# Self attention with one turn per entry, operands through a DRAM scratch, and the maxima rows laid in by transfer

## The reference, cut to what matters

```python
# 4 batch entries, 512 tokens, 128 features, 16 heads of 8
for l in range(N_LAYERS):                      # 4 layers
    h = rmsnorm(x, n1[l])
    q, k, v = jnp.split(h @ Wqkv[l].T + bqkv[l], 3, axis=-1)
    q = apply_rope(split_heads(q, H), cos, sin)
    k = apply_rope(split_heads(k, H), cos, sin)
    o = merge_heads(sdpa(q, k, split_heads(v, H), causal_bias)) @ Wo[l].T + bo[l]
    x = x + o
    # then a cross attention over 77 context tokens and a gated feed-forward
```

## Time and profile before

| | before |
|---|---|
| median of 3 runs | 2107.96 us |
| lowest to highest | 2101.96 to 2116.95 us |
| span of the profiled execution | 2100.9 us |
| TensorE busy in it | 1827.5 us (87%) |
| VectorE, ScalarE, GpSimd busy | 1415.5, 1067.7, 784.6 us |

### The profile page before, as it was taken

How to read it: one execution, slowest core, us unless ns; L and a number is a source line. 1 busy time by engine, 2 the same in 40 slices (tenths; PEclk the granted TensorE clock), 3 DMA queues, 4 the chain that set the end, 5 groups by cost and what they waited for, 6 DMA issues and landing times. The chain is left out here.

```text
span 2100.9 us, 34690 instructions
## 1 busy us (share of the span) xinstructions
PE 1827.5 (87%) x13011; PEld 1120.1 (53%) x13011; DVE 1415.5 (67%) x3427; ACT 1067.7 (51%) x1523; POOL 784.6 (37%) x1131
## 2 busy tenths in 40 slices
PE   5978998594777898899999999999999989989978
PEld 4557664373544444564544565644555554456557
DVE  8667776543676877864577885567786467787475
ACT  2655655131453566564466566366656446656510
POOL 4423324403624453431455342245443155443130
PEclk9999999597787898998999999999999999999989
DMA  7443333121000000141000033000014000003200
GB/s 227 111 137 101 109 104 97 63 69 39 21 1 13 1 1 13 37 110 43 16 1 1 1 93 84 28 1 1 1 44 120 14 16 2 1 26 99 52 1 21
DMA packets 69995, 100.91 MB, mean 48 GB/s; under 512 B 17126, under 2 KB 35438, under 8 KB 69188
## 3 DMA queue, kind: packets, MB, share of 16 engines
q1 hardware_dynamic: 60612, 90.01, 14.9%
q0 software_dynamic: 9216, 8.69, 1.6%
HBM read 52.43 MB, written 12.38 MB: 31 GB/s over the span
## 5 line engine op out<-in xcount | busy, mean ns | idle before, releaser
L1806 DVE TENSOR_REDUCE maxima<-wide 128x2 f32<-128x512 f32 (+3 forms) x512 | 406.1, 819 | 134.2 <-PE wide L836 130.7
L2042 ACT ACTIVATE prob<-wide 128x768 f32<-128x768 f32 (+1 forms) x384 | 332.2, 881 | 149.7 <-PE wide L836 149.4
L1965 ACT ACTIVATE prob<-wide 77x1024 f32<-77x1024 f32 x256 | 257.8, 1017 | 89.8 <-PE wide L836 86.5
L836 PE MATMUL wide<-q_g 32*128 32x256 f32 (+3 forms) x2048 | 268.5, 394 | 37.5 <-ACT prob L2042 18.1
L2284 POOL TENSOR_SCALAR_AFFINE_SELECT prob<-prob 128x256 f32<-128x256 f32 (+1 forms) x384 | 184.9, 487 | 296.4 <-ACT prob L2042 294.6
L1482 DVE TENSOR_REDUCE maxima<-wide 128x8 f32<-128x616 f32 x256 | 202.9, 795 | 110.7 <-PE wide L836 106.7
L836 PEld LDWEIGHTS wide<-q_g 32*128 32x128 f32 x2048 | 140.0, 188 | 205.6 <-issue 100.1
L2106 POOL TENSOR_TENSOR rstd<-moments,cst 128x4 f32<-128x4 f32 x88 | 90.4, 1027 | 360.7 <-DVE moments L1370 173.8
L1886 ACT ACTIVATE q_g<-wide 128x1024 fp32r<-128x1024 f32 x128 | 131.1, 1024 | 179.3 <-PE wide L836 177.4
L1886 ACT ACTIVATE q_g<-acc 128x512 fp32r<-128x512 f32 x192 | 114.5, 596 | 144.0 <-PE acc L836 139.0
L2191 POOL DMA_DIRECT2D masked_k<-kx x224 | 121.2, 546 | 177.4 <-PE wide L836 176.3
(11 more groups left out here) (253 smaller groups left out, 3096.1 us busy)
## 6 DMA issues: line engine op xcount, KB each, us to landing
masked_q<-q_g SPq DMA_DIRECT2D x448, 64.0 KB
masked_q<-mask_l SPq DMA_DIRECT2D x84, 308.0 KB
masked_k<-kx POOLq DMA_DIRECT2D x224, 19.5 KB, 1.9
A<-in_w SPq DMA_DIRECT2D x2, 2048.0 KB, 12.2
unit_w<-in_unit_w SPq DMA_DIRECT2D x8, 448.0 KB, 3.9
ffn_w<-in_ffn_w SPq DMA_DIRECT2D x4, 768.0 KB, 4.7
slots_in<-v_third SPq DMA_DIRECT2D x1, 2560.0 KB, 12.6
prob<-slots_in SPq DMA_DIRECT2D x8, 320.0 KB, 3.1
```

Source lines behind the costliest of these rows:

```text
L836: return e.matmul(out, lhsT, rhs, start=start, stop=stop, is_transpose=turn)
L1806: e.tensor_reduce(top[:, t, h], v[:, :, at0:at0 + P * t + P], AX.X, ALU.max, negate=True).then_inc(*made("max", *([("free", tile)] if t == ...
L1965: e.activation(p[0:SC, :], s[0:SC, :], ACT.Exp, bias=0.0, scale=1.0).then_inc(*made("exp", pb, ("free", tile)))
L2042: e.activation(pv, sv, ACT.Exp, bias=0.0, scale=8 ** -0.5).then_inc(*made("exp", pb, ("free", tile)))
```

## The change

Queries and keys are no longer expanded to 32 rows per head by token. The projection's columns are put in an order (`by_feature`: head in group, feature, group) in which 8 transposes turn a whole entry, all four groups, queries and keys (`qk_turn(l, b)`). ScalarE copies the result once, over the projection buffer; VectorE masks off the high part in one operation of 1024 columns and GpSimd subtracts the low part in one (`qk_cut`). Three transfers of 512 KB each then store the parts in a DRAM scratch `qk_rows` (`qk_store`), whose rows are in the layout of `q_g`, and each group's 512 KB are fetched from it into `q_g` (`qk_fetch`). A fourth of the scratch's rows, with the ones that the maxima multiply, is filled three times at the start of the program.

The maxima go into a small tile of 32 columns. `self_full` is one transpose of it, a ScalarE copy of 32x128, and a 16 KB transfer (`self_max`) into 8 rows of `q_g`. The transposed scores that need them begin at row 6 of `attend` instead of row 4, the fourth to sixth tile of them and all values move to `finish`, and output turns of an entry go to a fifth phase, `turn_out`.

```diff
+    def spread(b, *rows):
+        return in_rows(*zip(rows, (("qk_turn", l, b), ("qk_cut", l, b), ("qk_store", l, b))))
...
         if (l, b, g) == (0, 0, 0):
-            return in_rows((11, ("qk_turn", l, b, g)))
-        if (l, b) == (0, 0) and g < 3:
-
-            return beside(in_rows((8, ("qk_turn", l, b, g))),
-                          in_rows((0, ("stats", "s", l, 1)), (2, ("variance", "s", l, 1)), (4, ("apply", "s", l, 1)),
-                                  (8, ("turn", "s", l, 1)), (10, ("qkv", l, 1, 0)), (12, ("qkv", l, 1, 1)))
-                          if g == 1 else rotate(1, *[(k, 3 * k) for k in range(5)]))
-        if b == 0 and l:
-
-            return beside(in_rows((8, ("qk_turn", l, b, g))),
+            return in_rows((13, ("qk_fetch", l, b, g)))
+        phase, c = in_rows((4, ("qk_fetch", l, b, g))), b + 1
+        if (l, b) == (0, 0):
...
+                           rotate(1, (3, 1), (4, 4), (5, 7)),
+                           spread(1, 1, 4, 9)][g])
         if c < B:
@@ -361,29 +365,30 @@
 
     def attend(b, g):
         logits = lambda j, h0: ("self_logits", l, b, g, j, h0)
-        return in_rows((1, ("self_full", l, b, g)), (4, logits(0, 2)), (6, logits(0, 0)), (8, logits(1, 2)),
-                       (10, logits(1, 0)), (12, ("self_values", l, b, g, 0)))
+        return in_rows((1, ("self_full", l, b, g)), (2, ("self_max", l, b, g)), (6, logits(0, 0)), (8, logits(0, 2)), (10, logits(1, 0)))
 
     def finish(b, g):
-        logits, values = (lambda h0: ("self_logits", l, b, g, 2, h0)), (lambda j: ("self_values", l, b, g, j))
+        logits, values = (lambda j, h0: ("self_logits", l, b, g, j, h0)), (lambda j: ("self_values", l, b, g, j))
         if (b, g) == (B - 1, G - 1):
 
-            s = [(0, logits(2)), (0, logits(0)), (1, values(1)), (2, values(2)), (2, values(3))]
+            s = [(0, logits(1, 2)), (0, values(0)), (1, logits(2, 0)), (1, logits(2, 2)), (2, values(1)),
+                 (2, values(2)), (2, values(3))]
             s += [(2, ("o_out", "s", l, b, 1)), (4, ("o_turn", "s", l, b, 1)), (4, ("o_norm", "s", l, b, 1))]
             return in_rows(*s, (5, ("out_turn", "s", l, b)), (7, ("out_project", "s", l, b)))
-        s = [(0, logits(2)), (2, logits(0)), (4, values(1)), (8, values(2)), (10, values(3))]
-        if g % 2:
-            s += [(11, ("o_out", "s", l, b, g // 2)), (13, ("o_turn", "s", l, b, g // 2)), (13, ("o_norm", "s", l, b, g // 2))]
-        return in_rows(*s)
...
+    def turn_out(b, g):
+        s = [(8, ("o_turn", "s", l, b, g // 2)), (8, ("o_norm", "s", l, b, g // 2))]
+        return in_rows(*s, *([(10, ("out_turn", "s", l, b)), (12, ("out_project", "s", l, b))] if g == G - 1 else []))
+
+    items = [[prepare(b, g), scores(b, g), attend(b, g), finish(b, g)]
...
+                            io["qk_rows"].unsqueeze(0).broadcast_to([HG, PART, G * 2 * S])).then_inc(
+                    *landed("fill_qk_rows", ("qk_rows",)))
             yield
 
...
+            def qk_store(l, b):
+                held, t = ("qk_rows", l, b), parts(("sqt", l, b))
+                at = T.slot("qk_rows", held)
+                to = qk_rows[at][:, :].rearrange("(m x) c -> m x c", x=4)
+                for w in need(("sq_top", l, b), ("sq_cut", l, b), T.freed("qk_rows", held)):
+                    e.wait_ge(*w)
+                e.dma_start(to[:, 0, :], t[:, 1:3, :]).then_inc(*landed(f"store_qk{at}"))
+                e.dma_start(to[:, 1, :], t[:, 1::2, :]).then_inc(*landed(f"store_qk{at}"))
+                e.dma_start(to[:, 2, :], t[:, 0::2, :]).then_inc(
+                    *landed(f"store_qk{at}", ("qk_stored", l, b), ("free", ("sqt", l, b))))
+
+            def qk_fetch(l, b, g):
+                held = ("sq", l, b, g)
+                at, of = T.slot("q_g", held), qk_rows[T.slot("qk_rows", ("qk_rows", l, b))]
+                for w in need(("qk_stored", l, b), ("qk_rows",), T.freed("q_g", held)):
+                    e.wait_ge(*w)
+                e.dma_start(q_g[at][:, :, :].rearrange("p k s -> p (k s)").bitcast(F32), of[:, 2 * S * g:2 * S * g + 2 * S]).then_inc(
+                    *landed(f"fetch_qk{at}", ("sqk_copied", l, b, g), ("free", ("qk_rows", l, b))))
+
+            def self_max(l, b, g):
+                held, qk = ("mx_t", l, b, g), q_g[T.slot("q_g", ("sq", l, b, g))]
+                at = T.slot("mx_t", held)
+                for w in need(("mx_turned", l, b, g)):
+                    e.wait_ge(*w)
+                e.dma_start(qk[SELF_MAX:P:SELF_STEP, 0, :].bitcast(F32), mx_t[at].bitcast(F32)).then_inc(
+                    *landed(f"store_max{at}", ("sq_filled", l, b, g), ("free", held)))
 
...
-            def qk_turn(l, b, g):
-                tile = ("sqk_turn", l, b, g)
-                s = wide[T.slot("wide", tile)]
+            def qk_turn(l, b):
+                tile = ("sqk_turn", l, b)
+                s, src = wide[T.slot("wide", tile)], rope_b[:, :].rearrange("p (t k c) -> p t k c", t=NI, k=2)
                 for w in need(T.freed("wide", tile)):
                     e.wait_ge(*w)
                 stay_awake(s[:, 0:S], tile)
-                for w in need(("sq_cut", l, b), ("sk_cut", l, b)):
-                    e.wait_ge(*w)
-                turn_queries(s[:, 0:S], cut_queries(("sqt", l, b)), g)
-                turn_queries(s[:, S:2 * S], k_tok, g).then_inc(*made("q_turn", tile))
+                for w in need(("rotated", l, b)):
+                    e.wait_ge(*w)
+                for k in range(2):
+                    for t in range(NI):
+                        i_mm = mm(s[:, S * k + P * t:S * k + P * t + P], src[:, t, k, :], ident, turn=True)
+                i_mm.then_inc(*made("q_turn", tile))
 
...
@@ -1165,8 +1215,8 @@
                 stay_awake(a, tile)
                 for w in need(("smax_in", l, b, g)):
                     e.wait_ge(*w)
-                turn_queries(a, cut_queries(("sqt", l, b)), g).then_inc(
-                    *made("q_turn", tile, *([("free", ("sqt", l, b))] if g == G - 1 else [])))
+                mm(a[0:2 * HG * NI, 0:P], maxima_in[g % 2][:, :, :, :].rearrange("p i k t -> p (i k t)"), ident,
+                   turn=True).then_inc(*made("q_turn", tile))
 
...
-            def cut_q(l, b):
-                qt, src = cut_queries(("sqt", l, b)), rot[:, :, 0:16, :]
-                for w in need(own(), T.freed("hid", ("sqt", l, b)), ("rotated", l, b)):
-                    e.wait_ge(*w)
-                high_part(qt[:, :, :, 0:PART], src).then_inc(*made("cut", ("sq_top", l, b)))
-
-            def cut_k(l, b):
-                src = rot[:, :, 16:32, :]
-                before = ("sqk_turn", l, b - 1, G - 1) if b else ("sqk_turn", l - 1, B - 1, G - 1) if l else ("cleared",)
-                for w in need(own(), before):
-                    e.wait_ge(*w)
-                high_part(k_tok[:, :, :, 0:PART], src).then_inc(*made("cut", ("sk_top", l, b)))
+            def qk_cut(l, b):
+                high = parts(("sqt", l, b))[:, 1:3, :].rearrange("p k (c s) -> p (k c) s", c=2)
+                for w in need(("sq_raw", l, b), T.freed("hid", ("sqt", l, b))):
+                    e.wait_ge(*w)
+                high_part(high, raw_qk).then_inc(*made("cut", ("sq_top", l, b)))
...
                     at0 += P * t + P
                 if k == len(CAUSAL_TILES) - 1:
-                    fill_maxima(cut_queries(("sqt", l, b)), g).then_inc(*made("max_in", ("smax_in", l, b, g)))
+                    into = maxima_in[g % 2]
+                    for w in need(own()):
+                        e.wait_ge(*w)
+                    high_part(into[:, :, 0, :], top[:, :, :]).then_inc(*made("max_in"))
+                    for w in need(own()):
+                        e.wait_ge(*w)
+                    e.tensor_tensor(into[:, :, 1, :], top[:, :, :], into[:, :, 0, :], ALU.subtract).then_inc(
+                        *made("max_in", ("smax_in", l, b, g)))
...
-            def qk_turn(l, b, g):
-                tile, held = ("sqk_turn", l, b, g), ("sq", l, b, g)
-                s = wide[T.slot("wide", tile)]
-                for w in need(tile, T.freed("q_g", held)):
-                    e.wait_ge(*w)
-                copy(q_g[T.slot("q_g", held)][:, :, :].rearrange("p g s -> p (g s)"), s[:, :]).then_inc(
-                    *made("q", ("sqk_copied", l, b, g), ("free", tile)))
+            def qk_turn(l, b):
+                tile = ("sqk_turn", l, b)
+                for w in need(tile):
+                    e.wait_ge(*w)
+                copy(raw_qk, wide[T.slot("wide", tile)][:, :].rearrange("p (k c) -> p k c", c=2 * D)).then_inc(
+                    *made("q", ("sq_raw", l, b), ("free", tile)))
 
             def self_full(l, b, g):
-                tile = ("sq_full", l, b, g)
-                for w in need(tile):
-                    e.wait_ge(*w)
-                copy(q_g[T.slot("q_g", ("sq", l, b, g))][:, 0, :], acc[T.slot("acc", tile)][:, :]).then_inc(
```

(36 more changed lines are left out.)

111 lines of the change are left out of this document (65 added, 46 removed).

## The result

The changed kernel takes 2259.83 us (median of 4 runs, 2247.1 to 2282.64, the slowest of which counts as disturbed and is left out of the ratio) beside 2105.51 us of the kernel before (4 runs): 1.071 times the time before, 95% interval 1.066 to 1.076. It is slower by about 150 us, where 2078 us were predicted, in a range of 2045 to 2120.

The account below looks back on a forecast made before the run. The prediction took TensorE's own queue to set the pace, VectorE at three quarters of it. Its terms, -65 + 25 + 4 + 5 + 1 = -30 us, took 2107.96 to 2078 us, in a range of 2045 to 2120.

Parts of the forecast that it names:

- the steady part: Self-attention steps: -3.7 us per entry over 16 entries, -59 us, plus -6 in the slow clock: -65, bounds -83 to -11.
- +1.1 us per entry: At `self_full`: TensorE waits about 0.7 us for the maxima, 1.75 us per entry against 4 x 0.17 before.
- +4: First item of each layer: no finish phase beside it, so its maxima transfer is bare by about 1 us; 0 to 6.
- +5: Behind the layer entries: the pause lets the clock fall, 3.7 us in layer 3, 1.5 for the others; 0 to 14.
- The matmuls removed: Transposes of `qk_turn` and `self_full`: net 1.20 us saved per item, 77 us in all.
- -4.8: Us given back per entry of four items by the removed transposes, with TensorE's queue setting the pace.
- 11.4 to 10.5: Predicted fall, in us, of the distance from one `self_full` to the next in the profile after.
- The transfer of the maxima: From `self_full` to transposed scores: 2.7 us hidden behind 3.4; once per entry late behind stores, +0.5 per entry.
- (c): Rival: the maxima transfer is bare in every step, 1.3 us for each of 60 items, +78, about 2156 us; chance 0.12.
- The entries: Starts of layers: bare DRAM round trip delays first scores, 5.5 us into layers 1 to 3, 8.1 into layer 0; +25.
- Filling the scratch: Program start: 1.5 MB of filling lies behind weight loads nobody waits for yet; 0 to +2 us.
- (b): Rival: entries cost double, steps give half, clock low for longer (+14), -45 in the steps; about 2112 us, chance 0.2.

Follow-up runs that it names:

- e3: Changed kernel turning 32 columns of the identity in place of the maxima, so that wait is gone and the output differs: ratio 1.039 to the kernel before.
- e5: Changed kernel with the turn of the maxima one row later (step 2, transfer at 3) and the last values at step 12: 2205 us, ratio 1.055.
- e6: Kernel before with only the changed order of logits, values and output turns, all twelve transposes kept, no transfer: 2198 us, ratio 1.049.
- e7: e5 with the per-entry turn moved to step 4 and the turn of the normalised rows to step 2: 2140 us, ratio 1.023.
- e2: Changed kernel with nine 128x128 fp32 transposes added per item behind the wait for the maxima: 2239 us, ratio 1.061.
- e17: Changed kernel with nine matmuls of 32 rows added per item behind the wait for the maxima: ratio 1.125.
- e12: e7 with unread 128x512 bf16 matmuls added in the first entry of each layer alone: 2155 us, ratio 1.023.
- e13: Kernel before, in its old order, with only the 32-column turn and transfer of the maxima (two transfers an item): ratio 1.054.
- e15: e6 with its turn at step 2 and the last values at step 12: ratio 1.017 to the kernel before.
- e18: Changed kernel with eighteen matmuls of 32 rows added per item behind the wait for the maxima: ratio 1.195.
- e16: e12 with the old order, its logits shifted one step later, first values at step 12: ratio 1.040 to the kernel before.
- e9: Changed kernel with the old order of logits, values and outputs; per-entry turn, scratch and maxima transfer stay: 2176 us, ratio 1.029.

## Why the prediction was wrong

**The step that failed** is the steady part, "-59 us, and -6 in the slow clock", and in it above all one thing: the new wait at `self_full` was priced at its own length, "0.75", +1.1 us per entry. The four stages of self attention were to take 56 us less (-65, +4, +5); they took 114 more. The wait is as predicted. 26 of them sum to 19.9 us, 0.77 each, the plain ones 0.60 to 0.70. Its price was not its length. The prediction let the clock of layers 1 to 3 stand at 0.97 to 1.00 and gave it 5 us in all for falls behind the entries; it granted 0.66 to 0.75. Two causes meet: the order and the changed steps make more waits (3 falls become 18; e3, e5, e6, e7), and the transposes taken out are of the kind of work with which a fall is short (8 us become 21; e2 against e17). The earlier trace rows had shown a clock of 0.68 behind an entry, and the earlier trace rows 0.87 in layer 0; I read them as a matter of entries and not of every step.

**The matmuls removed**: right in number (576), too high in what they give back, and this is the second step that failed. The term "-4.8" per entry takes TensorE's queue for the pace of every step. Four steps in a row at the full clock with the wait for the maxima moved away show what it was worth. With a projection in them, the kernel before (layer 3) and e12 (in which three matmuls of filler, 0.66 us, are included):

```profile
1725.03:1771.11 46.08, 43.21 (x385) 22.47 (x385) 33.13 (x60) 30.13 (x45) 24.78 (x37) 1.00 0.01 2
1768.98:1814.32 45.34, 40.57 (x352) 19.06 (x350) 33.54 (x58) 26.67 (x41) 22.37 (x32) 1.00 0.23 81
```

Without one, the kernel before (layer 1) and e7:

```profile
1147.65:1191.94 44.29, 41.95 (x387) 22.55 (x387) 33.04 (x62) 28.94 (x37) 16.09 (x29) 1.00 0.00 1
1174.57:1214.47 39.90, 37.30 (x346) 17.71 (x342) 32.47 (x63) 23.84 (x32) 14.07 (x28) 1.00 0.20 61
```

An entry without a projection is 4.4 us shorter, one with it 0.7, or 1.4 less the filler: there TensorE idles 4.8 us in place of 2.9, in waits of up to 0.7 us each for VectorE to free scores and for ScalarE's exponentials and normalised rows. Three entries of a layer have a projection and one has none, so that the mean is some 2 us, not 4.8. In the changed kernel itself it is -0.27 a step in the last entry (above), for which the prediction has -0.93, its mean of -3.7/4; beside the wait for the maxima, those for exponentials, of which I let half go, stayed (0.25 and 0.29 us in one step). At 0.25 us a step even an undisturbed clock would have brought some 16 us in 64 items, an estimate, and not 59, and the sum near 2120 us. My "11.4 to 10.5" was the stage divided by 16, with entries in it.

**The order**: not priced. I counted what TensorE has left between the last causal scores and `self_full` and took 0.7 us from it, but did not ask what the moved values alone would do. That costs 104 us on the kernel before, and undoing it brings 88 of the 150 back on the kernel after.

**The transfer of the maxima**, hidden: right in this order (2.0 us of waits in the whole kernel after). Its rival (c) has the right mechanism in the old order alone (e13, 62 us).

**The waits for rotation and normalised rows**: missed. The per-entry turn stands at step 1 and waits 19.0 us in 12 times for GpSimd, the turn of the normalised rows 19.6 us (6.7 before). Moved, 65 us come back. I had looked at the entries between layers and not at the twelve other places of the new turn.

**The entries**, +25: right in sum, in part by luck. The three stretches between the layers took 4, 7 and 5 us more, 16 for 16.5 predicted; the first scores of layer 0 come 15 us later, of which 8 are there when the rotation ends (below), and 7 for 8.1 predicted. Fetches landed in 3.9 us (3.8 assumed). Stores landed in 3.8 each, and from the first of three to the issue of the fetch that waits for them 5.8 us passed (6.3 assumed):

```profile
q_g<-qk_rows SPq DMA_DIRECT2D x64, 512.0 KB, 3.9
...
qk_rows<-hid SPq DMA_DIRECT2D x48, 512.0 KB, 3.8
```

The split was off: TensorE waited 9.5 us for the first fetch of layer 0, but 1.5, 0 and 2.2 in layers 1 to 3, where 5 to 6 were predicted, since a down projection and the next projection stand there. What else lengthened those three stretches was not followed.

**Filling the scratch**, "0 to +2": wrong, about +8 to +11. Queue of SyncE, the kernel after:

```profile
15.22 2.11 SPq L736 DMA_DIRECT2D qk_rows<-in_qk_rows  x3
33.93 0.71 SPq L773 DMA_DIRECT2D mask_l<-masked_q  x2
48.79 0.30 SPq L784 DMA_DIRECT2D masked_q<-mask_l  x1
```

Before, the store of the masks was issued at 33.91 and the load that needs it at 37.99. Now the store is behind 1.5 MB of filling on its queue, and 1.5 MB that nobody waits for delayed a transfer that somebody does. TensorE's window of 40 to 60 us has 41 matmuls for 112. The fill was not moved in any run, so that its share is read from the two traces: 10 us more at 56 us into the program, 8 when the rotation for layer 0 ends.

**The rivals.** None let the clock fall in the steps; (b) came nearest in kind ("the clock low for longer", +14), behind the entries, though its sum took -45 of -65 where its name says half. The side on which the time came out had 0.15.

## What to carry to other kernels

A wait of TensorE costs what it does to the clock, and in the pairs of runs here that was two and a half to three and a half times its length (e3, e5, e7 against e5, e15 against e6): before taking matmuls out or moving them, look at the granted clock behind each short wait in the trace, and keep work between a producer's last piece and the first matmul that needs its result. Instructions that look like overhead (transposes over the full array) can be those with which a lowered clock comes back quickly; price their removal with the trace of a step at each level. What a removed matmul gives back is not its own time where other engines are nearly due: look at each kind of step, with and without the work of the next entry. When a change brings a new order along, run the old kernel with the new order alone first.

## What the runs showed of the hardware

TensorE busy 46 of 48 us did not yet bring the clock back from its lower level (e7, layer 1), when the work was mostly matmuls with 32 rows or 32 columns, nor did more such work (e17, e18: 15.5 and 29 us a stretch). Nine transposes of 128x128 fp32 an item, with 1.17 us at the full clock, shortened the stretches from 21 to 7 us, as did three bf16 matmuls of 128x512. Which property of these instructions does it was not told apart. Falls came behind waits as short as 0.6 to 0.7 us when several steps in a row had one (1223 to 1243 us above), and once a layer in e16 behind waits of 0.4 us and less. A single turn of 32 columns with a transfer of 16 KB into strided rows was hidden behind four steps (of 14) of about 0.7 us, and bare by 0.8 us a time at two (e9, layer 1).
